# Choosing the first 25 neighbours in natural blocks, with DMA turns and a pass through DRAM, in a 16-group neighbour-maximum kernel

## What is computed

```python
h = jnp.maximum(_layernorm(x, axis=-1), 0.0)
mask = A != 0
scores = jnp.where(mask, -jnp.arange(N, dtype=jnp.float32), neg_inf)
vals, idx = jax.lax.top_k(scores, S)            # S = 25
feats = jax.vmap(lambda x, i: x[i])(X, idx)     # X is h
agg = jnp.where(valid[..., None], feats, neg_inf).max(axis=2)
agg = jnp.where((degree <= S)[..., None], jnp.maximum(agg, 0.0), agg)
out = jax.nn.relu(jnp.einsum('bnf,fo->bno', jnp.concatenate([X, agg], axis=-1), W) + b)
x = x + out
```

## Time and profile before

| | |
|---|---|
| time, median of 3 runs | 699.86 us (698.64 to 700.08) |
| profiled execution: its own time | 697.45 us |
| profiled execution: its span | 695.7 us |
| TensorE, VectorE, ACT, POOL busy | 630.9, 613.7, 472.3, 50.3 us |
| HBM read, written | 42.08 MB, 4.19 MB |
| 16 DMA engines, share of the span | 25.7% |

### The profile page before, as it was taken

How to read it: one execution, slowest core, us unless ns; L and a number is a source line. 1 busy time by engine, 2 the same in 40 slices (tenths; PEclk the granted TensorE clock), 3 DMA queues, 4 the chain that set the end, 5 groups by cost and what they waited for, 6 DMA issues and landing times.

```text
span 695.7 us, 10819 instructions
## 1 busy us (share of the span) xinstructions
PE 630.9 (91%) x3376; PEld 297.4 (43%) x3376; DVE 613.7 (88%) x813; ACT 472.3 (68%) x642; POOL 50.3 (7%) x41
## 2 busy tenths in 40 slices
PE   2479998999989999899999999899999999999976
PEld 2133443535445354443545344353535335353423
DVE  3368999899998999989998899989998899988997
ACT  2689478783777639775795947777497927959120
POOL 1300021000210002100030002100021000300000
PEclk9899999999999999999999999999999999999999
DMA  9520141510415103251303313151122411020100
GB/s 361 199 87 27 60 152 68 182 70 16 152 73 200 60 15 136 83 188 60 128 23 122 151 60 151 68 196 57 41 122 87 185 60 32 16 107 1 60 15 16
DMA packets 19127, 67.64 MB, mean 97 GB/s; under 512 B 4499, under 2 KB 7830, under 8 KB 16534
## 3 DMA queue, kind: packets, MB, share of 16 engines
q1 hardware_dynamic: 19094, 67.26, 25.7%
HBM read 42.08 MB, written 4.19 MB: 67 GB/s over the span
## 4 chain that ended last, share of the span: by engine, by line
PE 66%; DVE 16%; issue 10%; ACT 4%; DVEq 1%; DMA 1%; POOL 1%; ACTq 0%
PE picked L506 18%; PE picked L507 17%; PE ring L455 14%; DVE late_hot L684 4%; PE side L469 4%; PE ring L449 4%; DVE hot L659 4%; PE side L463 4%; DVE best L775 3%; DVE best L678 3%; PE final L534 2%; PE final L538 2%; PE final L491 1%; DMA adj_in<-in_adj_dram 1%; DVEq L771 1%
## 5 line engine op out<-in xcount | busy, mean ns | idle before, releaser
L678 DVE TENSOR_TENSOR best<-picked,best 128x1024 f32<-128x1024 f32 x224 | 270.5, 1218 | 38.2 <-PE picked L507 36.0
L506 PE MATMUL picked<-hot,h_hi 128*128 128x512 f16 x512 | 194.5, 380 | 15.0 <-DVE best L775 7.5
L507 PE MATMUL picked<-hot,h_lo 128*128 128x512 f16 x512 | 194.0, 379 | 0.0
L506 PE MATMUL picked<-late_hot,hi_skew 128*128 128x512 f16 x336 | 127.6, 380 | 13.1 <-DVE late_hot L684 8.2
L507 PE MATMUL picked<-late_hot,lo_skew 128*128 128x512 f16 x336 | 127.3, 379 | 0.0
L344 ACT ACTIVATE late_rank<-ring,late_bias 128x512 bf16<-128x512 f32 x128 | 81.4, 690 | 57.6 <-PE ring L455 57.6
L775 DVE TENSOR_TENSOR best<-picked,best 128x1024 f32<-128x1024 f32 x84 | 102.4, 1219 | 8.3 <-PE picked L507 8.2
L378 ACT COPY best<-picked 128x1024 f32<-128x1024 f32 x32 | 32.2, 1013 | 102.6 <-PE picked L507 102.6
L659 DVE TENSOR_SCALAR hot<-rank 128x4096 f16<-128x4096 bf16 x64 | 89.4, 1399 | 12.0 <-ACT rank L344 12.0
L349 ACT ACTIVATE past<-side,bias_cut 128x512 bf16<-128x512 f32 x128 | 88.3, 690 | 6.2 <-PE side L469 4.9
L344 ACT ACTIVATE rank<-ring,bias_big 128x512 bf16<-128x512 f32 x128 | 83.1, 692 | 5.2 <-PE ring L455 4.9
(11 more groups left out here) (76 smaller groups left out, 562.1 us busy)
## 6 DMA issues: line engine op xcount, KB each, us to landing
adj_in<-in_adj_dram SPq DMA_DIRECT2D x16, 2048.0 KB, 7.7
late_skew<-late SPq DMA_DIRECT2D x32, 192.0 KB, 2.3
x_in<-in_x_dram SPq DMA_DIRECT2D x8, 512.0 KB, 8.5
xres<-in_x_dram SPq DMA_DIRECT2D x16, 256.0 KB, 7.8
late_skew<-late SPq DMA_DIRECT2D x16, 256.0 KB, 2.4
late_skew<-late SPq DMA_DIRECT2D x32, 128.0 KB, 2.0
out_dram<-xres SPq DMA_DIRECT2D x16, 256.0 KB, 2.0
late_skew<-late SPq DMA_DIRECT2D x32, 64.0 KB, 1.9
```

Of the source, the lines that this page charges most:

```text
L506: nc.tensor.matmul(dst, hi[:, slot, k, :], onehot, start=start, stop=False)
L507: return nc.tensor.matmul(dst, lo[:, slot, k, :], onehot, start=False, stop=stop)
L678: nc.vector.tensor_tensor(best[:, half, s, :, :], picked[s][:, :, :], best[:, half, s, :, :], ALU.max).then_inc(picked_read, 1)
```

## The change

The first 25 are no longer chosen in the classes but in natural blocks: block k holds the columns 128k to 128k + 127.

- `mask_t` comes from four DMA transposes of 128 x 1024 a group, issued by SP (`turn_masks`). The 32 transposes on TensorE and ACT's four copies are gone.
- `place` replaces lower and prefix sums and the past: for block k a matmul with `select_w` (upto less 64 on the diagonal) and, before it, one with `rest_w` (ones less `select_w`) that completes block k - 1, 15 matmuls a group. ACT takes the sign as `chosen`, +1 for a chosen neighbour and -1 otherwise. It is again a chain of 8 links.
- SP stores `chosen` to the DRAM tensor `kept` by block, 8 DMAs of 128 KB, and loads it by class as `picks`, one of 1 MB, when the stores have landed.
- `ranks` has one matmul to a class, over `picks`.
- The pipeline is one group deeper: in the step of g behind uses 4 to 11 stand the choosing of g + 2 and the ranks of g + 1. The masks of g + 3 are made at the end of the step, all four by ACT.
- The late ranks of g + 1 and their count stand behind the rounds of g, between and behind uses 2 and 3 of g + 1 and the projection, and `count_rounds` behind `finish_group`. The count goes to `side`, not to `final`. ACT waits for the fold before it writes `late_rank`.
- The halves of the next batch are made at use 13 and the flags at uses 12 and 14; before, both stood behind use 15.
- At the start x is loaded first and the `adj` of group 0 in quarters; VectorE makes the halves of batch 0. Ahead of the loop stand now the choosing of groups 0 and 1 and late ranks and count of group 0.

```diff
-    LATE_WITH, PREFIX_WITH, RANK_WITH = spread_over(5, 8), spread_over(5, 12), spread_over(9, 13)
-
-    LATE_HOT_USES, COUNT_USE, MASK_USES = (10, 11), 9, (4, 9)
+    SELECT_WITH, RANK_WITH = spread_over(4, 11), spread_over(4, 11)
+
+    FLAG_USES, RELU_USE, LATE_HOT_USES = (12, 14), 13, (7, 9)
...
+            def turn_masks():
+
+                sp.reg_add(masks_due, masks_due, Q)
+                for q in range(Q):
+                    sp.wait_ge(mask_made, q + 1)
+                    if q == 0:
+                        sp.wait_ge(mask_made, masks_due)
+                    sp.dma_start_transpose(mask_t[:, :, q * P:(q + 1) * P], mask[:, q, :]).then_inc(mask_turned, 16)
...
+            def store_chosen(first):
+
+                for k in range(K):
+                    sp.reg_add(chosen_due, chosen_due, 1)
+                    if k == 0 and not first:
+                        sp.wait_ge(picks_loaded, picks_due)
+                    sp.wait_ge(chosen_made, chosen_due)
+                    sp.dma_start(kept_by_block[k], chosen[:, k, :]).then_inc(chosen_stored, 16)
+
+            def load_picks(ranked):
+
+                sp.reg_add(stored_due, stored_due, LANDED)
+                sp.reg_add(picks_due, picks_due, 16)
+                if ranked is not None:
+                    sp.wait_ge(ring_read, ranked)
+                sp.wait_ge(chosen_stored, stored_due)
+                sp.dma_start(picks[:, :, :], kept_by_class).then_inc(picks_loaded, 16)
...
+            def choose(g, k):
+
+                if k == 0 and not (isinstance(g, int) and g == 0):
+                    act.wait_ge(chosen_stored, LANDED * g)
+                act.wait_ge(place_written, g * K + k + 1)
+                nc.scalar.activation(chosen[:, k, :], side[:, :], ACT.Sign, bias=bias_cut[:, 0:1], scale=-1.0).then_inc(chosen_made, 1)
...
                 if more:
                     for s in range(2):
                         first_maxima(g + 1, s, (u + 1) % 2)
-                if not at_end(it, u, 2):
-                    for n in range(TURNS):
-                        turned_mask(at + TURN_AT, n)
+                    act.wait_ge(fold_step, g + 1)
+                    for k in range(K):
+                        stage(at + LATE_AT, k, late_rank, late_bias[:, k:k + 1])
...
+            def place(g, k, counted):
+
+                if k == 0:
+                    pe.wait_ge(mask_turned, TURNED * (g + 1))
+                    if counted is not None:
+                        pe.wait_ge(late_reduced, counted)
+                else:
+                    pe.wait_ge(chosen_made, g * K + k)
+                    nc.tensor.matmul(side[:, :], rest_w[:, :], mask_t[:, k - 1, :], start=False, stop=True, skip_group_check=True)
+                nc.tensor.matmul(side[:, :], select_w[:, :], mask_t[:, k, :], start=(k == 0), stop=True,
+                                 skip_group_check=True).then_inc(place_written, 1)
 
             def ranks(g, at, k):
 
-                pe.wait_ge(past_made, g * K + k + 1)
-                accumulate(at, k, [(rank_w, mask_t[:, k, :]), (minus_w, past[:, k, :])])
+                if k == 0:
+                    pe.wait_ge(picks_loaded, 16 * (g + 1))
+                accumulate(at, k, [(half_w, picks[:, k, :])])
...
             for use in range(PAIRS):
                 pick_pair(0, use, 0)
-            for n in range(TURNS):
-                turn_mask(1, FIRST_RING - TURNS, n)
             pe.wait_ge(h_turned, 2)
+            for k in range(K):
+                place(1, k, None)
+            for k in range(K):
+                late_ranks(0, LATE_AT, k)
+            pe.wait_ge(chosen_made, 2 * K)
+            count(0)
...
                 if more:
+                    late_ranks(g + 1, at + LATE_AT, 0)
+                    late_ranks(g + 1, at + LATE_AT, 1)
                     pick_pair(g + 1, 2, next_slot)
+                    late_ranks(g + 1, at + LATE_AT, 2)
+                    late_ranks(g + 1, at + LATE_AT, 3)
+                    pick_pair(g + 1, 3, next_slot)
+                project(g, it, u, new_batch)
+                if more:
+                    for k in range(HALF, K):
+                        late_ranks(g + 1, at + LATE_AT, k)
+                    if not at_end(it, u, 2):
+                        pe.wait_ge(chosen_made, K * (g + 3))
+                    count(g + 1)
...
                 finish_group(g, s, 16 * (it * (UNROLL // 2) + u // 2 + 1))
+                if more:
+                    count_rounds(g + 1, 1 - s)
```

More of the change, by code:

```diff
@@ L24 @@
 I32 = mybir.dt.int32
+U32 = mybir.dt.uint32
 ALU = mybir.AluOpType
@@ L253, in _ @@
             load_xres(0, 0)
-            for g in (0, 1):
-                sp.wait_ge(mask_made, Q * (g + 1))
-                load_adj(g + 2, g)
+            sp.reg_add(masks_due, masks_due, Q)
+            for q in range(Q):
+                sp.wait_ge(mask_made, q + 1)
+                sp.dma_start_transpose(mask_t[:, :, q * P:(q + 1) * P], mask[:, q, :]).then_inc(mask_turned, 16)
+            load_adj(2, 0)
+            store_chosen(True)
+            load_picks(None)
+            turn_masks()
+            load_adj(3, 1)
             skew_h(0, 0)
             skew_late(0)
+            store_chosen(False)
+            load_picks(K)
+            turn_masks()
             def step(it, u):
@@ L441, in take @@
                     pe.wait_ge(ring_read, at - 1)
-            def turn_mask(g, at, n):
-                if n == 0:
-                    pe.wait_ge(mask_made, Q * (g + 1))
-                take(at + n)
-                for j in range(2):
-                    for q in range(Q):
-                        last = nc.tensor.transpose(ring16[n % 2][:, j, q * P:(q + 1) * P], mask[:, q, 2 * n + j::K], eye[:, :])
-                last.then_inc(ring_written, 1)
             def accumulate(at, k, terms):
@@ L497, in turn_h @@
                 for n, bank in enumerate((side, final)):
-                    if n == 1 and not first:
-                        pe.wait_ge(rounds_known, 2 * batch)
+                    if n == 0:
+                        pe.wait_ge(chosen_made, K if first else K * (2 * batch + 1))
+                    elif not first:
+                        pe.wait_ge(result_made, 2 * batch)
                     for j in range(4):
@@ L577, in step @@
                     pick_pair(g, use, slot)
-                    if use == PAIRS and more:
-                        lower_sums(at - TURNS)
-                    for k in LATE_WITH[use]:
-                        late_ranks(g, at + LATE_AT, k)
-                    if K - 1 in LATE_WITH[use]:
-                        count(g)
-                    for k in PREFIX_WITH[use] if more else []:
-                        prefix_sums(g + 1, k)
+                    for k in SELECT_WITH[use] if not at_end(it, u, 2) else []:
+                        place(g + 2, k, (CHAINS + 1) * g + 1)
                     for k in RANK_WITH[use] if more else []:
```

219 lines of the change are left out of this document (108 added, 111 removed).

## The result

The change is slower. The kernel after took 753.89 us (median of 4 runs, 752.55 to 756.99), the kernel before 699.25 beside it: a ratio of 1.079, 95% interval 1.0757 to 1.0822. The forecast was 725 within 702 to 752: the right side, less than half the size (25 us of 54.6), and the time is outside the range. The profiled execution took 756.99 us around a span of 755.3, so it is read against the 697.45 and 695.7 of before: 59.6 us more. It is the slowest of its four, and so this is 5 us more than the medians are apart.

A forecast was written before the change was run, and what follows sets the result against it. TensorE bounds uses 4 to 15, VectorE the rounds and behind them. Profiled 697.45 us, plus 30 at the start, less 5 in the loop, gives 722.5; plus 2.4 to the median gives 725 us, range 702 to 752.

The forecast's parts named there:

- the one on DMA: SP's queue in odd groups: four turns behind 21 skewing DMAs, 1.0 us each, landing in time, so no stall.
- S: The start of VectorE's maximum of use 4, from which the prediction counts times in a group.
- the limit of 1.2: The SP time in us each turn may take in odd groups for its result to land by use 4.
- Rival 1: Turns are slow, 2.3 us each: 4.4 us late in 7 groups, start loses 10 more, 766 us; chance 0.13.
- the first sign of being wrong: The prediction is wrong if TensorE waits for turned masks in the loop.
- The 16.9 of the even stretches: Uses 4 to 15 of even groups take 16.9 us against 21.23 before, 4.3 saved in each of 8 groups.
- the 34.4 of the sum: The gain entered in the loop's sum for uses 4 to 15 of eight groups, 8 x 4.3 us.
- The tail: Behind the rounds: late ranks and count delay VectorE's next maximum, 3.7 us lost, 15 times.
- rival 2: TensorE runs through behind the rounds without waiting for a bank, giving back 30 us: 695 us, faster; chance 0.10.
- Odd groups: Uses 4 to 15 take 19.4 us against 21.44; with a shorter hot, 3.7 us saved in each of 7 groups.
- The start: Before the loop: turned masks and choosing chains bring group 1's hot at 100 us, 30 lost, bounds +19 to +45.
- Rival 3: Gain and loss cancel: a start at +19 and a loop at -17 meet at 702 us; chance 0.03.

The follow-up runs named there:

- copies_not_turns: The changed kernel with each DMA turn replaced by a plain DMA copy of the same 256 KB: 784.18 us, one run, with 51 rounds and not 42.
- turns_first: The changed kernel with SyncE's four turns issued ahead of the 14 skewing DMAs of h: 739.70 us, ratio 1.0579.
- turns_first_no_loop: The kernel turns_first with every step written out, so no engine jumps back: 732.09 us, ratio 1.0486.
- late_half_next: The changed kernel with late ranks 4 to 7 and the count moved into uses 4 and 5 of the next stretch: 753.27 us, ratio 1.0801.
- turns_first_early_masks: The kernel turns_first with the masks of group 2 made at the start by VectorE, not ACT: 727.77 us, ratio 1.0404.
- first_picks_direct: The kernel turns_first_early_masks with group 0's ranks summed from the choices in SBUF, not through DRAM: 743.65 us, with eight rounds in group 0 instead of three.
- use 12 against 11: The kernel before with ACT's halves of the next batch moved from behind use 15: behind use 12 692.32 us (0.9905), behind use 11 699.16 us (1.0005).

## Why the prediction was right or wrong

**The step that failed** is the one on DMA, "I take 1.0, nearer to the first since the queue takes the next before the last has landed: no stall." Turns from S + 31.5, four of 1.0 us and 2.0 for landing had the mask there at S + 37.5, 0.8 us before it was wanted. Two terms were too small. The turns start at S + 34.4 (S + 33.6 from group 5 on), since the flags are skewed from S + 20.2 on and not 17.8: ACT makes the second pair of flags behind the halves of h. And four turns take the queue 5.4 us (1.33 each by the median, past the limit of 1.2 too). The landing was right: 2.0 us behind the last issue (170.21 to 172.19). So the mask is there at S + 41.7 and was wanted at S + 39.2. At 1.0 us a turn it would still have come 1.2 us late in group 2 and 0.4 in group 6: the place in the queue weighs more than the turning, as copies_not_turns shows. Rival 1 had the stall, but put it down to slow turns of 2.3 us. turns_first takes the wait out of every group of the loop and 14.2 us off the time. A margin of 0.8 us, on which all the even groups hung, was no ground for "no stall". TensorE waiting for turned masks in the loop is also the first sign of being wrong that the prediction named.

**The 16.9 of the even stretches** was right where nothing stands in the way: 16.35 in group 14, 16.43 in three groups of turns_first. It is the mean of groups 2 to 14 that came to 20.1, and with group 15 the eight stretches gained 10.5 us, not the 34.4 of the sum. The half clock behind the waits of groups 2, 4, 8 and 12 was not in the sum at all.

**The jump** was in no step. TensorE's waits and VectorE's order were followed in the rows, but not what ACT does at the first instruction of a pass. The trace of before had it, as two short idle times of ACT put down to issue, 2.8 us in all. Taken out of turns_first it gives 7.6 us back (turns_first_no_loop).

**The tail**, 3.7 us, 15 times: 10.86 against 11.1, so 3.4 us, and the 2 us of waiting for the count. Right, and rival 2 (no waits, a gain) fell. late_half_next names its owner, and shows that the loss can't be had back whole: VectorE's 1.5 us for the rounds only move into a stretch where it is the bound (16.23 us busy of 16.42 in turns_first), and the late ranks add waits for picks.

**Odd groups**: 19.4 right; the hot 2.00 and not 1.22, 0.8 us in each of 7. POOL begins its subtraction only at 149.51 (in turns_first), 1.2 us ahead of the hot, because ACT makes the first flags, 2.2 us, ahead of the halves.

**The start**, +37 and not +30, inside its bounds of +19 to +45. The links were at the upper bound (1.81) through the first chain, whose matmuls have the length of half clock, and in the last five links of the second; the picks for group 0 came at 42.85; and the masks of group 2 were turned in 5.4 us, not 4.0. What follows the maximum of use 5 took 16.9 and not 15.7. turns_first_early_masks takes 6.6 of it back, first_picks_direct 3.0.

Together: start +7, even stretches +24, odd hots +5.5, tail -3 make 33.5 of the 34.6 us by which the profiled spans (59.6) miss the forecast (25). Rival 3 (loss and gain cancel) was far off.

What stays open: why ACT's pause at the jump is 1.24 us in one kernel, 2.37 or 4.85 in others and 8.55 in late_half_next, and at what point TensorE's clock falls: all the cases here are waits of different lengths in different places.

## What to carry to other kernels

Work that leaves the compute engines for a DMA queue has a deadline: add up everything ahead of it in that queue, what the first of these waits for and all of its landing, and call a margin of less than a microsecond a stall until it is measured. Before a loop's jump, look at what each engine does first behind it; an answer that another engine wants at once should not stand there. And a repair moved one step further can cost what it won (use 12 against 11), so measure both neighbours.

## What was not expected of the hardware

- Turning a 128 x 1024 bf16 block by DMA lands in 3.3 us (median of 60), a plain copy of it in 4.1; the turn costs its queue 1.33 us, the copy 0.71. The 42 us a group worked out from the Trainium skill ("VectorE: DVE Perf Modes", The three transpose paths) did not come: four turns take the queue 5.4 us. What the Trainium skill says in "Advanced Engine Details and Errata", X-Bar Transpose, is borne out in the landing, not in the queue.
- ACT's first instruction behind a jump came 4.85 us late in turns_first, 2.37 in turns_first_early_masks, whose program of ACT is four masks shorter ahead of the loop, and 1.24 in the kernel before.
- TensorE's granted clock fell to half (1.2 GHz) in waits of 2.57 and 5.46 us (groups 2 and 12 of the changed kernel), for 3.4 and 6.8 us, and stayed at 2.4 GHz in those of 1.80 and 1.90 (groups 6, 10). In groups 4 and 8, behind the jump, it fell 1.0 and 1.3 us after waits of 2.58 and 1.98 had ended, where TensorE waits again, for ACT's choice, and stayed down for 6.8. VectorE waited 3.51 us in group 2 against 1.48 in group 6: 0.8 us more of TensorE's waiting made 2.0 of VectorE's.
- A pass of VectorE over the hot takes 1.22 us alone, 1.9 to 2.9 beside POOL's subtraction.
